# Deformable preact block on one Trainium2 core: the deform stage on four bands of whole rows

## The chip, the cores and the metric

The kernel runs on one core of a Trainium2 chip. The metric is the device time of one execution in microseconds (us). The core has TensorE (PE: matmuls, with its weight loads shown as PEld), VectorE (DVE), ScalarE (ACT), GpSimd (POOL), and SyncE (SP), which here only issues DMAs; ScalarE issues a few as well. A "q" behind an engine's name in a row (SPq, ACTq) is that engine's sequencer, busy with issuing a DMA.

## The reference, cut to what matters

The input is 8 images of 32 channels, 128 x 128, fp32. Two residual layers follow each other:

```
x = x + pointwise/attention mixes of depthwise3x3(gn(x))      # one 3x3 convolution once the weights are folded
x = x + conv3x3(deform(gn(x)), w_conv) + b_conv

deform(x): off = conv3x3(x, w_off)           # 64 channels: (row, column) offsets
           rows, cols = clip(grid + off)     # own pixel plus an offset
           bilinear mix of the pixels (floor, ceil) of rows and cols
```

`gn` is a normalization with as many groups as channels: one mean and one variance for each channel of each image. The kernel folds it into the weights and a bias, so that every padding pixel must hold the channel's mean. As long as every offset is below 1 in size, the bilinear mix needs only the own pixel, its neighbour above or below and its neighbour at the left or right; a general path, which these inputs don't take, stands behind the fast one.

## The kernel before

Each image is stored as `[128 partitions, 32 or 33 blocks, 130 columns]`: partition 32*q + c holds channel c of the image rows 4*b + q, b being the block. Three such tiles (`x1a`, used in turn) hold the result of the first convolution, `x1b` the same shifted by two rows (one convolution needs both, each matmul contracts four rows of 32 channels), `xa` and `xb` the input of the first convolution, `mapa` and `mapb` the deformed image, input of the second. A convolution of an image is 8 groups of 4 blocks. [...]

The program goes over images i = 0 to 7, and in each over 8 chunks k. In chunk k TensorE computes the offsets of one eighth of image i (`offsets`, L715, 24 records), and behind them the jobs that `jobs_behind` lists: groups of the first convolution of image i+1 (`conv1_groups`, at chunks 0 to 3), and the eight groups m = 0 to 7 of the second convolution of image i-1 (`LAST_CONV2`: one behind chunk 3, one behind chunk 4, two behind each later chunk). `CONV2_GROUPS` says which group of blocks the m-th is. All these jobs share three PSUM banks in turn, so a job waits for the bank to be emptied three jobs earlier. The jobs before the last image keep this order; the last image has its own (`END_CONV2`, `END_GROUPS`).

The deform stage of chunk k runs through three engines. Its input is `x1_quads`: the image cut in four quarters (left or right half, upper or lower half), one for each 32 partitions, with one row of neighbours around. ScalarE copies row differences and column neighbours into place (`offset_parts`, L909 and L911), waits for the offsets, and writes their positive parts and absolute values (L920 to L924); VectorE selects and multiplies (`deform`, L1317 to L1329); GpSimd adds up (L1115 to L1127) and writes `mapped`, then computes the row differences for the chunk after next (`row_steps`, L1101). So chunk k needs, on ScalarE, what GpSimd did behind chunk k-2. TensorE may start the offsets of chunk k when VectorE is done with chunk k-2 (`off_used`).

SyncE moves the data between these layouts, in one queue and in the order of the code:

- `copy_x1b` (L402): `x1a` into `x1b`, shifted, 520 KB each, two for each half of the image
- `move_quads` (L336): `x1a` into `x1_quads`, 16 DMAs for each half, rows of 65 or 64 elements
- `move_mapa` (L407): `mapped` into `mapa`, 16 DMAs for each half, rows of 64 elements
- `copy_mapb` (L417): `mapa` into `mapb`, two for each half, once `move_mapa` of that half has landed
- `load_xb` (L392), the input of image i+2, 8 DMAs; `store` (L364), 5 and 4 DMAs

Within image i the order is: `copy_x1b` half 1, `copy_mapb` half 0, `store` part 1, `move_quads` half 1, `move_mapa` half 1, `copy_mapb` half 1, `load_xb`, then for the next image `copy_x1b` half 0 and `move_quads` half 0, then `move_mapa` half 0 and `store` part 0. The conv2 jobs wait at m = 0 for half 0 of `mapb` and at m = 2 (chunk 5, block group 0) for half 1 (L675).

The padding columns are written by ScalarE: in `x1a` and `x1b` (`pad_x1`, L811) and in `mapa` (`pad_map`, L828). The mean comes from `x1_norm` on VectorE, which stands ahead of the chunk that follows the last first-convolution group. `clamp` (L935) repeats the edge rows and columns in `x1_quads`. For the last image the lower quarter rows don't go by DMA: `end_row` copies (L298) on VectorE, ScalarE and GpSimd write `xa` and `xb` in two parts.

## Time and profile before

| | us |
|---|---|
| median of 3 runs | 739.05 (738.85 to 739.9) |
| the profiled execution, its own time | 740.63 |
| its span, first to last instruction | 738.8 |
| TensorE busy | 690.1 (93%) |
| VectorE, ScalarE, GpSimd busy | 519.5, 475.7, 491.6 |
| mean granted TensorE clock | 0.981 |
| DMA packets | 240878, of which 140880 under 512 B |

The page is one profiled execution. Busy times are unions of an engine's instructions. A row of a timeline begins with its start and its length in us; "[4.13 <-DMA ...]" is idle time of the engine just before, and what ended it. A row of windows gives busy time and, in brackets, instructions for each engine, then the granted clock as a share of 2.4 GHz.

### The profile page before, as it was taken

Reading aid. Unit: us, or ns where it says so; the run is one execution under the profiler, and the core shown is the slowest. Engines: PE = TensorE matmul, PEld = TensorE weight load, DVE = VectorE, ACT = ScalarE, POOL = GpSimd, SP = SyncE. Lnnn points to the kernel's source line nnn. Section 1 sums busy time; section 2 is a strip of 40 time slices with the busy share of each in tenths; the row PEclk is TensorE's granted clock in tenths of the full one; section 3 lists DMA queues with packets and bytes.
Section 4 is the critical chain, followed back from the end, with each engine's and each line's share of the span. In section 5 each row is a group of like instructions: output and inputs, shape, how many; then the busy total and the mean of one; then the engine's idle time right before and its main releaser. Section 6 shows DMA issues by size and latency. Waiting matters only on the chain. (4 is left out here: it accounts for less than half of the span.)

```text
span 738.8 us, 10814 instructions
## 1 busy us (share of the span) xinstructions
PE 690.1 (93%) x3500; PEld 247.4 (33%) x3500; DVE 519.5 (70%) x1031; ACT 475.7 (64%) x841; POOL 491.6 (67%) x434
## 2 busy tenths in 40 slices
PE   4799989999999889998999979999899999997966
PEld 4333333333333233333333333333333333332322
DVE  3687996598954886749955698566985595657592
ACT  7487867785675836676467654667576674876560
POOL 4004968879687486766686575857766849699650
PEclk9999989999999989999999999999999999999998
DMA  8969904999789894989959799696968563657554
GB/s 141 186 102 148 177 10 104 205 145 197 136 195 180 148 200 104 232 146 170 184 133 238 133 166 166 155 220 122 204 127 190 140 148 66 160 109 166 133 123 112
DMA packets 240878, 113.08 MB, mean 153 GB/s; under 512 B 140880, under 2 KB 235184, under 8 KB 239024
## 3 DMA queue, kind: packets, MB, share of 16 engines
q1 hardware_dynamic: 216784, 100.55, 71.0%
q10 hardware_dynamic: 24032, 11.78, 8.4%
q8 instruction: 29, 0.48, 0.3%
q14 instruction: 33, 0.27, 0.1%
HBM read 31.59 MB, written 16.78 MB: 65 GB/s over the span
## 5 line engine op out<-in xcount | busy, mean ns | idle before, releaser
L1317 DVE COPY_PREDICATED other_row<-down_ps,row_diff 128x768 f32<-128x768 int32 x128 | 124.4, 1024 | 139.4 <-ACT down_ps L920 139.1
L715 PE MATMUL off_ps<-x1a,wo 128*64 128x512 f32 x768 | 178.9, 601 | 2.1 <-DVE other_row L1329 2.1
L1115 POOL TENSOR_TENSOR other_row<-other_row,x_quads 128x512 f32<-128x512 f32 x64 | 76.3, 1193 | 154.2 <-DVE other_row L1329 154.2
L715 PE MATMUL off_ps<-x1b,wo 128*64 128x512 f32 x768 | 175.9, 593 | 0.0
L606 PE MATMUL c_ps<-xb,w 128*64 128x512 f32 x336 | 150.8, 598 | 5.6 <-DVE x1a L1301 5.5
L606 PE MATMUL c_ps<-mapb,w 128*64 128x512 f32 x336 | 151.7, 595 | 0.0
L608 PE MATMUL c_ps<-xa,w 128*64 128x512 f32 x336 | 150.8, 598 | 0.0
L909 ACT ACTIVATE other_row<-row_diff 128x768 f32<-128x768 f32 x128 | 101.7, 843 | 68.2 <-POOL row_diff L1101 63.0
L608 PE MATMUL c_ps<-mapa,w 128*64 128x512 f32 x294 | 132.7, 595 | 0.0
L1101 POOL TENSOR_TENSOR row_diff<-x_quads 128x594 f32<-128x594 f32 x64 | 79.5, 1243 | 43.7 <-ACT x_quads L945 43.7
L920 ACT ACTIVATE down_ps<-off_ps,bias_o 128x512 f32<-128x512 f32 x64 | 41.7, 652 | 84.1 <-PE off_ps L715 75.6
L715 PEld LDWEIGHTS off_ps<-x1b,wo 128*64 128x64 f32 x768 | 55.5, 136 | 110.2 <-issue 110.2
L715 PEld LDWEIGHTS off_ps<-x1a,wo 128*64 128x64 f32 x768 | 54.4, 138 | 103.7 <-issue 100.7
L1121 POOL TENSOR_TENSOR other_col<-other_col,off_abs 128x512 f32<-128x512 f32 x64 | 83.0, 1297 | 5.0
L1118 POOL TENSOR_TENSOR other_col<-other_col,other_row 128x512 f32<-128x512 f32 x64 | 81.8, 1279 | 5.0
L1127 POOL TENSOR_TENSOR mapped<-other_col,other_row 128x512 f32<-128x512 f32 x64 | 81.8, 1278 | 5.0
L1116 POOL TENSOR_TENSOR other_col<-other_col,other_row 128x512 f32<-128x512 f32 x64 | 81.9, 1280 | 0.0
L606 PEld LDWEIGHTS c_ps<-xb,w 128*64 128x64 f32 x336 | 45.3, 137 | 100.7 <-issue 94.3
L606 PEld LDWEIGHTS c_ps<-mapb,w 128*64 128x64 f32 x336 | 44.7, 136 | 90.5 <-issue 89.9
L932 ACT ACTIVATE beyond<-off_abs,minus_one 128x1024 bf16<-128x1024 f32 x64 | 73.0, 1140 | 0.1
L922 ACT ACTIVATE off_abs<-off_ps,bias_o 128x1024 f32<-128x1024 f32 x64 | 70.7, 1105 | 0.0
L1274 DVE BATCH_NORM_STATS2 stats<-x1a 128x6 f32<-128x512 f32 x64 | 42.1, 683 | 24.3 <-ACT x1a L868 24.3
(134 smaller groups left out, 970.4 us busy)
## 6 DMA issues: line engine op xcount, KB each, us to landing
x1b<-x1a SPq DMA_DIRECT2D x28, 520.0 KB, 7.6
mapb<-mapa SPq DMA_DIRECT2D x28, 520.0 KB, 6.9
mapa<-mapped SPq DMA_DIRECT2D x224, 64.0 KB, 2.1
out_dram<-x1a SPq DMA_DIRECT2D x49, 256.0 KB, 4.7
x_quads<-x1a SPq DMA_DIRECT2D x192, 65.0 KB, 3.1
xb<-in_x_dram SPq DMA_DIRECT2D x48, 256.0 KB, 8.1
xa<-in_x_dram ACTq DMA_DIRECT2D x40, 256.0 KB, 6.8
xa<-in_x_dram SPq DMA_DIRECT2D x16, 256.0 KB, 6.9
```

The source lines that it names most:

```text
L606: nc.tensor.matmul(bank[0:64, :], weights[:, kx, :], rows_b[:, 4 * g:4 * g + 4, kx:kx + W], start=(kx == 0), stop=(kx == 2))
L608: last = nc.tensor.matmul(bank[64:128, :], weights[:, kx, :], rows_a[:, 4 * g:4 * g + 4, kx:kx + W], start=(kx == 0), stop=(kx == 2))
L715: last = nc.tensor.matmul(off_ps[k % 2][64 * t:64 * t + 64, CH * n:CH * n + CH], wo[wpar][:, kx, 64 * t:64 * t + 64], rows[:, 4 * k:4 * k ...
L909: act.activation(other_row[n][:, :, KR // 2 * odd:KR // 2 * odd + KR // 2, :], every_other_3(row_diff[n], odd), ACT.Copy)
L932: act.activation(beyond[:, :], off_abs[k % 2][:, :], ACT.Relu, bias=minus_one[:, :], accum_out=far[i % 2][:, k:k + 1]).then_inc(beyond_rea ...
L1101: pool.tensor_tensor(row_diff[n][:, :, :], x1_quads[:, KR * k + 1:KR * k + KR + 2, :], x1_quads[:, KR * k:KR * k + KR + 1, :], ALU.subtrac ...
L1115: step(pool.tensor_tensor(split(column), split(column), own, ALU.add))
L1116: step(pool.tensor_tensor(side, side, other_row[n][:, 0, :, :], ALU.add))
L1118: step(pool.tensor_tensor(side, side, column, ALU.subtract))
L1121: step(pool.tensor_tensor(side, side, off_abs[n][:, 1:2 * CH:2].rearrange("p (h w) -> p h w", h=KR), ALU.mult))
L1127: pool.tensor_tensor(by_pairs(mapped, KR * k, 0), split(side), split(column), ALU.add).then_inc(mapped_ready, 1)
L1317: last = dve.copy_predicated(other_row[n][:, :, KR // 2 * odd:KR // 2 * odd + KR // 2, :], bass.AP(tensor=rows.tensor, offset=rows.offset ...
```

## The change

- `x1_quads` becomes `x1_strips`: four bands of 32 whole rows, one for each 32 partitions, half 0 (rows 0 to 15 of each band) in one buffer and half 1 in two that take turns. Rows are stored by remainder modulo 4, so that each of the 16 DMAs of a half moves one contiguous run of 4 or 5 whole rows with their pads (520 B each) for each partition. The rows' pads must be written before: `copy_x1b` and the strips of image i+1 now wait for `x1_pads` of that image, and `pad_x1` moves to the chunk behind the first convolution's last group.
- A chunk is now 8 rows by one half of the width: chunks 0 to 3 are rows 0 to 15 of all bands, 4 to 7 the others. Both halves' strips of image i+1 are issued in one go of 32 DMAs during image i, ahead of `move_mapa` half 0; none is left between the last chunk and `move_mapa` half 1.
- `mapped` has the layout `[4 rows, 8 blocks, 130]` and carries the pad columns (`pad_mapped`), so `move_mapa` moves 2080 B runs. Its halves are now blocks 0 to 3 and 4 to 7 of each band.
- For images 0 to 5, conv2's m = 0 waits for both halves of `mapb`, and the order is block groups 0, 2, 4, 6, 1, 3, 5, 7. For images 6 and 7 a group is 4 blocks 8 apart; m = 0 needs half 0 and m = 3 half 1.
- `row_steps` computes the differences of two chunks in two instructions (128x792 and 128x330), behind each even chunk; ScalarE waits for both.
- `SECOND_CONV1` puts the last two conv1 groups behind chunks 2 and 3 in place of both behind chunk 2.
- At the end, five conv2 groups of image 6 stand in the chunks (seven before), three behind them (one before). For image 7, three groups need half 0; the other five need the left columns by DMA and one part of `end_row` copies (12 ScalarE, 10 GpSimd, 10 VectorE).
- Biases use 64-column sums, and some small tiles lie in spare room of the strips. The scratch for GpSimd's own DMAs is cut; this kernel issues none there.

```diff
-    SECOND_CONV1 = [[3], [4, 5], [6, 7], [], [], [], [], []]
+    SECOND_CONV1 = [[3], [4, 5], [6], [7], [], [], [], []]
-    END_CONV2 = [[], [], [0], [1], [], [2, 3], [4, 5], [6]]
-    CONV2_GROUPS = [1, 5, 0, 4, 2, 6, 3, 7]
-    STORE_AFTER = [7, 8]
-    END_GROUPS = [1, 5, 2, 6, 3, 0, 4, 7]
-    END_PARTS = [0, 0, 1, 1, 2, 2, 2, 2]
+    END_CONV2 = [[], [], [0], [1], [2], [3], [4], []]
+    CONV2_GROUPS = [0, 2, 4, 6, 1, 3, 5, 7]
+    STORE_AFTER = [6, 8]
+    BEFORE_END_GROUPS = [1, 2, 3, 0, 4, 5, 6, 7]
+    END_GROUPS = [1, 2, 3, 4, 5, 6, 7, 0]
+    END_PARTS = [0, 0, 0, 1, 1, 1, 1, 1]
@@ SyncE
                 if prev:
                     sp.wait_ge(mapped_ready, NK * i)
-                    move_quads(sp, i % 3, 1)
                     if i >= 2:
                         sp.wait_ge(conv2_done, 8 * (i - 1))
+                    sp.wait_ge(mapped_pads, 2 * i)
                     move_mapa(1)
                     sp.wait_ge(mapa_moved[1], A_MOVES * DMA * i)
                     copy_mapb(1)
...
-                    sp.wait_ge(x1_ready, 8 * (i + 1) + 5)
+                    sp.wait_ge(x1_pads, i + 2)
                     sp.wait_ge(off_done, NK * i + 4)
                     copy_x1b((i + 1) % 3, 0)
-                    sp.wait_ge(x1_ready, 8 * (i + 1) + 8)
-                    sp.wait_ge(mapped_ready, NK * i + 5)
-                    move_quads(sp, (i + 1) % 3, 0)
+                    sp.wait_ge(mapped_ready, NK * i + 4)
+                    for half in range(2):
+                        move_strips(sp, i + 1, half)
...
+                    move_rows(xa, 0, 4, end_moved[0])
+                    sp.wait_ge(end_moved[0], A_MOVES * DMA)
+                    copy_rows(xb, xa, 0, 4, end_copied[0])
+                    sp.wait_ge(mapped_pads, 2 * i + 2)
+                    sp.wait_ge(mapped_ready, NK * i + 6)
+                    move_left_columns(end_moved[1])
+                    sp.wait_ge(end_moved[1], A_MOVES * DMA)
+                    copy_rows(xb, xa, 4, 4, end_copied[1])
@@ TensorE
-                if m in (0, 2):
+                halves = [m // 3] if spread(i) and m in (0, 3) else range(2) if not spread(i) and m == 0 else []
+                for half in halves:
@@ ScalarE
-                act.wait_ge(diff_ready, g + 1)
+                act.wait_ge(diff_ready, 2 * (g // 2 + 1))
...
+                    if nxt and k and 7 in conv1_groups(i, k - 1):
+                        pad_x1(i + 1, (i + 1) % 3)
@@ GpSimd
+                pool.tensor_tensor(diff[:, 0:12 * WQP].rearrange("p (q j w) -> p q j w", q=3, j=4),
+                                   rows(PLANE, inner), rows(0, inner), ALU.subtract).then_inc(diff_ready, 1)
+                pool.tensor_tensor(diff[:, 12 * WQP:17 * WQP].rearrange("p (j w) -> p j w", j=5),
+                                   rows(0, [[WP, 5]]), rows(strip_row(-1), [[WP, 5]]),
+                                   ALU.subtract).then_inc(diff_ready, 1)
...
-                    if k + 2 < NK:
-                        row_steps(i, k + 2)
-                    elif i + 1 < NB:
-                        row_steps(i + 1, k + 2 - NK)
+                    if k % 2 == 0 and k < NK - 2:
+                        row_steps(i, k // 2 + 1)
+                    elif k == NK - 2 and i + 1 < NB:
+                        row_steps(i + 1, 0)
@@ VectorE
+            def copy_end_rows():
+                dve.wait_ge(end_copied[1], B_MOVES * DMA)
+                dve.wait_ge(mapped_ready, NK * NB)
...
             for m in range(8):
-                if m == 2:
-                    copy_end_rows(1)
+                if m == COPY_END_BEFORE:
+                    copy_end_rows()
```

`COPY_END_BEFORE` is 3. The strips of one band:

```python
STRIP_PLANES = ((0, 0, 5), (1, 0, 4), (2, 0, 4), (3, -1, 5))
def move_strip(queue, i, half, strip):
    par, to = i % 3, strips_of(i, half)
    p_to = Q * (2 * (strip % 2) + strip // 2)
    for q, first, n in STRIP_PLANES:
        p, b = (Q * (q + 1), NJ * strip + 4 * half + first) if q < 3 else (0, NJ * strip + 4 * half + first + 1)
        at = PLANE * q + WP * first
        if i > 0:
            queue.dma_start(to[p_to:p_to + Q, at:at + n * WP],
                            x1a[par][p:p + Q, b:b + n, :].rearrange("p b w -> p (b w)")).then_inc(strips_loaded[half], DMA)
```

## Rows read from the trace of the kernel before

**Rows 1.** The page's part 1, busy time of each engine

```profile
PE 690.1 (93%) x3500; PEld 247.4 (33%) x3500; DVE 519.5 (70%) x1031; ACT 475.7 (64%) x841; POOL 491.6 (67%) x434
```

**Rows 2.** TensorE's waits: who waited for whom, total us, times, longest

```profile
PE c_ps L616 <- DMA mapb<-mapa: 15.5, 6, 4.1
PE c_ps L633 <- DVE w L1270: 8.2, 2, 5.1
PE c_ps L606 <- DVE x1a L1301: 5.5, 1, 5.5
```

**Rows 3.** Windows: busy PE, PEld, DVE, ACT, POOL (instructions), granted clock, DMA, GB/s

```profile
261.00:271.00 10.00, 10.00 (x54) 4.10 (x48) 7.98 (x14) 2.12 (x3) 9.61 (x9) 0.72 1.26 198
...
437.00:442.00 5.00, 5.00 (x32) 2.45 (x26) 4.89 (x8) 0.00 (x0) 4.84 (x5) 0.66 1.25 191
```

**Rows 4.** TensorE's timeline around the second convolution's groups, images 1, 4, 5 and 6

```profile
157.08 0.59 PE L606 MATMUL c_ps<-mapb,w 128*64 128x512 f32 x1
...
416.61 0.59 PE L606 MATMUL c_ps<-mapb,w 128*64 128x512 f32 x1
...
436.36 0.48 PE L616 MATMUL c_ps<-mapb,w 128*32 128x384 f32 x1 [4.13 <-DMA mapb<-mapa]
...
505.83 0.59 PE L606 MATMUL c_ps<-mapb,w 128*64 128x512 f32 x1
...
591.33 0.59 PE L606 MATMUL c_ps<-mapb,w 128*64 128x512 f32 x1
```

**Rows 5.** SyncE's timeline from 440 to 530 us, one period of its queue

```profile
442.66 14.53 SPq L349 DMA_DIRECT2D x_quads<-x1a  x16
457.28 11.64 SPq L414 DMA_DIRECT2D mapa<-mapped  x16
...
485.64 13.24 SPq L349 DMA_DIRECT2D x_quads<-x1a  x16
...
516.72 0.62 SPq L425 DMA_DIRECT2D mapb<-mapa  x1
```

**Rows 6.** By line: L414's issue times (min/median/max ns), L414's and L425's landing times

```profile
L414 SPq DMA_DIRECT2D mapa<-mapped x224: 585/611/1875, 118.6 to 665.8; - x112
...
DMA to landing us min/median/max: 2.1/2.1/7.3
...
DMA to landing us min/median/max: 6.5/7.6/11.4
```

**Rows 7.** Timelines of VectorE and ScalarE around chunk 3 to 4 of image 4

```profile
422.78 0.73 DVE L1301 SCALAR_TENSOR_TENSOR x1a<-c_ps,bias,x1a 128x512 f32<-128x512 f32 x1
...
426.86 1.14 ACT L932 ACTIVATE beyond<-off_abs,minus_one 128x1024 bf16<-128x1024 f32 x1
```

**Rows 8.** Timelines of GpSimd, ScalarE and VectorE in image 0

```profile
72.33 1.23 POOL L1101 TENSOR_TENSOR row_diff<-x_quads 128x594 f32<-128x594 f32 x1
...
76.50 1.94 DVE L1317 COPY_PREDICATED other_row<-down_ps,row_diff 128x768 f32<-128x768 int32 x2
...
86.50 1.28 POOL L1127 TENSOR_TENSOR mapped<-other_col,other_row 128x512 f32<-128x512 f32 x1
...
105.27 0.66 ACT L920 ACTIVATE down_ps<-off_ps,bias_o 128x512 f32<-128x512 f32 x1 [5.76 <-PE off_ps L715]
```

**Rows 9.** Timelines of TensorE, GpSimd and VectorE in the last image

```profile
632.93 2.75 PE L715 MATMUL off_ps<-x1a,wo 128*64 128x512 f32 x12
635.51 2.75 PE L715 MATMUL off_ps<-x1b,wo 128*64 128x512 f32 x12
...
649.05 1.27 POOL L1127 TENSOR_TENSOR mapped<-other_col,other_row 128x512 f32<-128x512 f32 x1
...
710.52 0.40 POOL L1138 COPY xb<-mapped 32x256 f32<-32x256 f32 x1
...
711.52 0.43 DVE L1385 TENSOR_SCALAR xa<-mapped,ones 32x256 f32<-32x256 f32 x1
...
732.43 0.20 PE L738 MATMUL c_ps<-far_image,ones 128*1 128x8 f32 x2 [0.92 <-DVE far_image L1398]
```

455 lines of the change are left out of this document (233 added, 222 removed).

## The prediction, on record before the changed kernel was run

> **What bounds the kernel now.** I read the page's busy times first: TensorE works 690.1 of 738.8 us [rows 1], so a change gains only where TensorE waits. Its waits by releaser come next [rows 2]: six waits, 15.5 us in all, for `mapb`, always at L616, block group 0, which is m = 2 behind chunk 5; two, 8.2 us, for the scaled weights of the first convolution at the start; one of 5.5 us near the end. Then the clock, window by window: after the 4.1 us wait of image 2 the granted clock is 0.72 of 2.4 GHz for 10 us, after that of image 4 it is 0.66 for 5 us [rows 3]. TensorE was fully busy there, so these cost 10 x 0.28 = 2.8 us and 5 x 0.34 = 1.7 us more. Last the timeline [rows 4]: m = 0 of the second convolution starts at 416.61 in image 4 and at 505.83 in image 5, 89.2 us apart; less the wait of 4.13 and 1.7 of slow clock a period of TensorE's own work is 83.4 us. From 157.08 (image 1) to 591.33 (image 6) are 434.2 us, five periods are 417.0, so 17.2 us are lost in images 1 to 5. That is what the change can reach in the middle of the kernel.
>
> Why `mapb` is late is in SyncE's queue [rows 5]. From `move_quads` half 0 at 442.66, which the strips replace, to `copy_mapb` half 1 (second issue at 516.72, landed some 6.7 us later, 523.4) are 80.8 us with scarcely a pause: 16 moves in 14.5, 16 in 11.6, then stores and copies until 485.64, then 16 and 16 more. An issue takes 0.61 us whatever the size [rows 6], 0.65 with the gap. The chain then starts anew only after the 8 loads of x and `copy_x1b`. So SyncE's queue is as long as TensorE's period, and the wait is its excess.
>
> **The steady images.** *Removed:* the 16 moves between chunk 7 and `move_mapa` half 1, 13.2 us [rows 5]. *Moved:* they now stand ahead of `move_mapa` half 0, so the queue holds the same 64 moves and they come only from one place to another. Each is still an issue of 0.65 us. What is saved is the queueing: 14.5 and 11.6 us for 16 where 10.4 is the bare price. I take 32 strips at 20.9 us. *Moved earlier:* both halves of `mapb` are needed at m = 0, behind chunk 3, instead of the second at m = 2, behind chunk 5. That is two groups and two chunks of offsets sooner: a group is 12 records and starts 2.57 us before what follows it (the two halves of a chunk's offsets start 2.58 apart [rows 9]), so 2 x 2.57 + 2 x 5.15 = 15.4 us.
>
> *Added:* SyncE waits for `x1_pads` before `copy_x1b`, with the strips, `move_mapa`, stores and all the rest queued behind it. The pads stand on ScalarE behind chunk 4's parts, and the mean they use comes from `x1_norm`, which on VectorE stands behind the addition of m = 0 (that order can be seen at 422.78, where L1301 is followed by the norm [rows 7]). So a loop closes: m = 0, its addition and the norm, pads, SyncE's queue, `mapb`, the next m = 0. Its length decides. Let S be the start of m = 0:
> - group 0 takes 2.7, chunk 4's offsets 5.2, ScalarE's parts 2.5, `sum_far` 1.3 (from 424.5, the end of those offsets, `sum_far` starts at 426.86 [rows 7]), three pads 0.9: S + 12.7. VectorE's mean is ready before (0.7 addition, 2.7 norm).
> - two issues of `copy_x1b` 1.3, strips 20.9, `move_mapa` half 0 10.4: S + 45.3.
> - stores, `copy_x1b` half 1, `copy_mapb` half 0, as now from 468.9 to 485.64: 16.7 [rows 5]: S + 62.0.
> - `move_mapa` half 1 10.5, last landing 2.1 after its issue at best, 7.3 at worst [rows 6]; loads of x by ScalarE fall here, I take 3.6: S + 75.5.
> - `copy_mapb`: second issue 0.7 later, landing 6.5 at best, 7.6 the median [rows 6], I take 6.8 as before a load of x: S + 83.0.
> TensorE comes back to m = 0 at S + 83.4. The loop fits by 0.4 us. With landings at their worst it is 3 to 4 us too long, with issues slightly cheaper it is 2 short. I take 0.4 us of waiting for each of images 2 to 6, 2 us in all, bounds 0 and 15. Waits this short leave the clock alone: of the 17.2 us now lost, waits are 12.7 (15.5 less the last image's 2.8 [rows 2]) and the two slow stretches 4.5, so the short waits of images 1, 3 and 5 cost no clock.
>
> **Image 1.** Here the queue starts late. Before, `copy_x1b` for image 1 went out at chunk 4 of image 0; now it waits for pads behind chunk 5. ScalarE's parts of chunk 5 start at 105.27 [rows 8]; I add 1.2 (below), 2.5 parts, 0.3 for the new `pad_mapped`, 1.3 `sum_far`, 0.9 pads: 111.4. Then 1.3, strips 20.9, `move_mapa` half 0 10.4: 144.0; `copy_x1b` 1.3, landing, `copy_mapb` half 0 1.5: 146.8; no stores yet; `move_mapa` half 1 10.5 and landing 1.5: 158.8; `copy_mapb` 0.7 + 6.5: 166.0. TensorE wants m = 0 at 157.08 [rows 4] + 1.2 = 158.3 (the new `SECOND_CONV1` leaves that place where it is). So a wait of 7.7 us that was 0.5, and a slow clock behind it: 2.8 by [rows 3] (1.7 the other bound). Image 1 costs 10.5 us.
>
> **Image 0 and the pairs.** ScalarE's copies for an even chunk wait for two differences instead of one. A difference of 594 elements takes 1.23 [rows 8]; 792 and 330 elements in proportion 1.65 and 0.7, so the pair is ready 1.1 us later than the one is now. Where the deform stage runs without slack the way from `mapped` of chunk k-2 to that of chunk k is 72.33 to 87.78, 15.4 us [rows 8]; it becomes 16.6 for two chunks. Chunk 2 of image 0 has it once before `x_norm` of image 2, so the first wait for weights (3.1 of the 8.2 [rows 2]) grows by 1.2 us. GpSimd's work doesn't grow (2.35 for two chunks against 2.46), and in images 1 to 6 a chunk of TensorE is 10.3 us or more, which hides it; if that cover is gone it is 0.6 us a chunk. *Edits with one answer, no cost:* strips in other layouts (same elements), 64-column bias sums, pads in `mapped` (2 x 0.3 on ScalarE, which has slack), `clamp` of half 1 no longer waiting for its DMA.
>
> **The last image**, T being its first offsets, 632.93, and TensorE's end about 731.5, T + 98.6 [rows 9]. `mapped` of chunk 0 ends at T + 17.4 [rows 9]. With 16.6 a pair chunk 5 is ready at T + 17.4 + 33.2 + 8.8 = T + 59.4. Then 16 left columns 10.4, landing 1.5, `copy_rows` 0.7 + 6.4 at the low end of the landings: T + 78.5. Now the end copies: ScalarE's 12 at 0.43 are 5.1; GpSimd's 10 at 0.40 and VectorE's 10 at 0.43 beside each other [rows 9] are 4.4. Group 4 of 8 starts at T + 83.8. Before it TensorE has been idle some 10 us, where it waited 5.5 [rows 2]. Five groups, 4 x 2.57 + 2.7 = 13.0, and 2.8 of slow clock: T + 99.6. That is 1.0 later than now; between 97 and 103, as landings go. What I count here replaces the waits that the last image has now (2.8 for `mapb`, 2.1 for VectorE, and the 5.5).
>
> One rule speaks against the shared end copies: the Trainium skill, SBUF — State Buffer, "SBUF: two separate sides", says that VectorE in a two-port mode and GpSimd hold one port pair by an exclusive lock for a whole instruction. By that the two shares of ten would add up to 8.3 us, 3.2 over the 5.1 of ScalarE. In this trace a GpSimd copy (0.40) and a VectorE copy (0.43) ran side by side in the same stretch, so the trace doesn't bear it out for these copies.
>
> **The sum**, against the span of 738.8: -17.2 (images 1 to 5), +10.5 (image 1), +2.0 (images 2 to 6), +1.2 (image 0), +1.0 (last image) = -2.5, a span of 736.3. The profiled execution took 740.63 by its own time, 1.8 above its span, and the runs' median is 739.05; 739.05 - 2.5 gives 736.5 us.
>
> **The rivals.**
> - *The loop is longer than TensorE's period.* The mechanism is the one above: `copy_x1b` waits for pads that wait for m = 0. It decides from a loop of 83.4 us. For it: landings of `move_mapa` reach 7.3 and of `copy_mapb` 11.4 [rows 6], and ScalarE's loads fall right there. Against it: the strips are short runs no more, and the queue gets 5 us of rest before. With 86 us in each of five images, 2.6 us each, 13 for 2, it is 747.5; 750 if one wait drags the clock down. Chance 0.28. This one is slower than before.
> - *The queue gets shorter than counted.* Moves of one run for each partition could issue below 0.61, say at 0.55; 64 of them and 48 in image 1's way save 3.5 us in each loop: images 2 to 6 wait nothing (-2), image 1 3 less, the tail 1 less: 730.5. For it: only that quads with many rows took up to 14.5 for 16. Against: `mapa` moves take 0.61 in all their 224. Chance 0.14.
> - *The wait moves and nothing else.* The 17.2 us come back as image 1's and small waits in full: 739. Chance 0.10.
> - *The lock of the shared port pair holds* in the end copies: the 3.2 us above lengthen the idle stretch before the last five groups, 739.7. Chance 0.02.
>
> **How the numbers follow.** Forecast 736.5 with chance 0.46, its own range 732.5 to 741. A measurement tells about 0.2% from no change, so 737.6 to 740.5 counts as the same. Faster: 0.14, and two thirds of 0.46, 0.31: 0.45. Same: the third left of it less what passes 740.5, 0.12, and 0.10 and 0.02: 0.24. Slower: 0.28 and 0.03: 0.31. The range 729 to 749 leaves out the far ends of the two outer cases, 0.2 together.
>
> **What would show it.** Right: no wait at L616 for images 2 to 6, or below 1 us; one wait of 6 to 9 us at the first group of image 1's m = 0, with a lower clock behind it; 32 strips in a row in about 21 us; an idle TensorE of about 10 us in the last image; m = 0 to m = 0 in 83.4 to 84 us. Wrong: periods above 85 us with `mapb` as releaser each time (the loop), waits of TensorE for VectorE's L1329 in images 0 or 7 (the pairs), or issues of strips far from 0.61 us.

## The result and the profile after

The changed kernel takes 779.23 us (median of 5 runs, 775.46 to 779.66), the kernel before 739.36 beside it (5 runs, 738.85 to 740.16): a ratio of 1.0528, 95% interval 1.0502 to 1.0553. The forecast was 736.5 with a range of 729 to 749; it was wrong in sign and in size. The execution that was profiled took 775.46 us, the lowest of the five (that of the kernel before 740.63), so the trace shows 34 to 35 us of the loss and not the whole 40.

The page's busy times and the waits of the kernel after (waiting engine and line, releaser, total us, times, longest) answer to [rows 1] and [rows 2]. L662 is the first group of m = 0, L651 any other group, L448 is `copy_x1b`, L842 a pad, L1364 the addition of m = 0, L1065 an end copy:

```profile
PE 697.6 (90%) x3500; PEld 249.3 (32%) x3500; DVE 507.7 (66%) x1017; ACT 458.5 (59%) x792; POOL 491.0 (63%) x434
...
DVE x1a L1364 <- PE c_ps L670: 54.1, 7, 16.5
...
PE c_ps L662 <- DMA mapb<-mapa: 34.9, 6, 15.0
...
PE c_ps L651 <- ACT xb L1065: 8.3, 1, 8.3
...
SPq L448 <- ACT x1a L842: 78.6, 7, 26.0
```

TensorE waits for `mapb` at each of the six m = 0, 34.9 us in all, and 2.6 us once more in the last image; before it was six waits with 15.5 us in all, at m = 2. New is the last line: ahead of `copy_x1b` SyncE stands still for the pads, 78.6 us in all. Of this 26.0 are in image 0 (where before it stood still for 23.2 us too, for `mapped`), and 5.3 to 10.8 in each of images 1 to 5. In these its queue isn't full, it is held up.

TensorE's timeline at the first group of m = 0, images 1 to 6, against [rows 4]:

```profile
176.77 0.82 PE L662 MATMUL c_ps<-mapb,w 128*32 128x384 f32 x1 [15.04 <-DMA mapb<-mapa]
...
267.81 0.82 PE L662 MATMUL c_ps<-mapb,w 128*32 128x384 f32 x1 [5.65 <-DMA mapb<-mapa]
...
357.15 0.48 PE L662 MATMUL c_ps<-mapb,w 128*32 128x384 f32 x1 [3.39 <-DMA mapb<-mapa]
...
445.81 0.48 PE L662 MATMUL c_ps<-mapb,w 128*32 128x384 f32 x1 [3.46 <-DMA mapb<-mapa]
...
536.56 0.82 PE L662 MATMUL c_ps<-mapb,w 128*32 128x384 f32 x1 [5.58 <-DMA mapb<-mapa]
...
624.66 0.48 PE L662 MATMUL c_ps<-mapb,w 128*32 128x384 f32 x1 [1.75 <-DMA mapb<-mapa]
```

The six starts split the loss into three parts (TensorE's last matmul ends at 732.63 before and 766.91 after):

| | before | after | measured | forecast |
|---|---|---|---|---|
| start to m = 0 of image 1 | 157.1 | 176.8 | +19.7 | +8.9 |
| from there to m = 0 of image 6 | 434.2 | 447.9 | +13.7 | -12.4 |
| from there to TensorE's end | 141.3 | 142.2 | +0.9 | +1.0 |
| sum | | | +34.3 | -2.5 |

(Forecast of the second line: -17.2, + 2.8 for the clock behind image 1's wait, + 2.0.) The last image came out as forecast, the other two did not. A period is 88.1 to 91.0 us where TensorE's own work is 83.4.

Windows behind the waits, as in [rows 3] (busy time of PE, PEld, DVE, ACT, POOL, granted clock, DMA, GB/s):

```profile
176.00:181.00 5.00, 4.23 (x28) 2.14 (x29) 0.00 (x0) 0.00 (x0) 0.00 (x0) 0.54 1.24 197
...
267.00:277.00 10.00, 9.19 (x50) 4.06 (x52) 3.05 (x16) 1.50 (x3) 1.91 (x2) 0.71 1.26 185
...
445.00:451.00 6.00, 5.18 (x34) 2.63 (x36) 0.63 (x2) 2.10 (x3) 5.04 (x4) 0.72 1.26 195
```

In the 5 us with the end of the 15.0 us wait TensorE was granted 0.54 of 2.4 GHz (most of that time the level of 1.2), in the 6 us with the end of the 3.5 us wait 0.72. In the first two stretches VectorE, ScalarE and GpSimd have little or nothing to do: the whole chain of engines has run dry behind m = 0.

One round of SyncE's queue, from image 3's m = 0 at 357.15 to image 4's at 445.81, against [rows 5]:

```profile
371.39 0.61 SPq L448 DMA_DIRECT2D x1b<-x1a  x1
...
372.69 23.89 SPq L375 DMA_DIRECT2D x_strips<-x1a  x32
396.69 10.18 SPq L456 DMA_DIRECT2D mapa<-mapped  x16
406.91 2.27 SPq L407 DMA_DIRECT2D out_dram<-x1a  x3
...
411.94 0.90 SPq L448 DMA_DIRECT2D x1b<-x1a  x1
...
413.76 1.72 SPq L469 DMA_DIRECT2D mapb<-mapa  x1
...
417.82 5.67 SPq L407 DMA_DIRECT2D out_dram<-x1a  x3
...
424.17 12.11 SPq L456 DMA_DIRECT2D mapa<-mapped  x16
437.69 0.65 SPq L469 DMA_DIRECT2D mapb<-mapa  x1
...
439.06 15.66 SPq L438 DMA_DIRECT2D xb<-in_x_dram  x8
460.01 0.60 SPq L448 DMA_DIRECT2D x1b<-x1a  x1
```

The round can be read off leg by leg, with the forecast's terms beside it:

| leg | measured | forecast |
|---|---|---|
| m = 0 to `copy_x1b` (357.15 to 371.39) | 14.2 | 12.7 |
| its two issues, to 372.69 | 1.3 | 1.3 |
| 32 strips, to 396.69 | 24.0 | 20.9 |
| `move_mapa` half 0, to 406.91 | 10.2 | 10.4 |
| stores, `copy_x1b` half 1, `copy_mapb` half 0, to 424.17 | 17.3 | 16.7 |
| `move_mapa` half 1 and its landing, to 437.69 | 13.5 | 13.5 |
| `copy_mapb` half 1, to m = 0 of the next image at 445.81 | 8.1 | 7.5 |
| round | 88.7 | 83.0 |

The first leg on ScalarE in the round that starts at 445.81: parts of chunk 4, `sum_far`, pads, and SyncE's 460.01 above follows at once:

```profile
455.61 0.66 ACT L966 ACTIVATE down_ps<-off_ps,bias_o 128x512 f32<-128x512 f32 x1 [8.42 <-PE off_ps L762]
...
457.92 1.14 ACT L978 ACTIVATE beyond<-off_abs,minus_one 128x1024 bf16<-128x1024 f32 x1
...
459.06 0.92 ACT L842 ACTIVATE x1a<-dve_columns 128x66 f32<-128x66 f32 x3
```

Chunk 4's offsets are there 9.8 us behind m = 0; 7.9 were counted. The low clock behind the wait makes them late, so the wait lengthens the loop that causes it. The other images show by how much. Behind image 6's m = 0, which waited only 1.75 us, the granted clock is 1.00 and `copy_x1b` follows after 12.5 us (624.66 to 637.20), as forecast; at a clock of 0.72 (images 3 and 4) it follows after 14.2, at 0.51 (image 5) after 15.4.

### The profile page after: what moved, and what is told of

It reads as the page before. It is cut to its first block, busy times and chain, and to the rows that moved or that the text cites. A ratio compares the mean times of both kernels' runs of the same rounds, so it can differ in the third digit from the quotient of the medians.

```text
span 773.5 us, 10713 instructions
## 1 busy us (share of the span) xinstructions
PE 697.6 (90%) x3500; PEld 249.3 (32%) x3500; DVE 507.7 (66%) x1017; ACT 458.5 (59%) x792; POOL 491.0 (63%) x434
## 4 chain that ended last, share of the span: by engine, by line
SPq 45%; PE 14%; DMA 9%; POOL 6%; issue 4%; ACT 4%; DVE 3%; ACTq 0%; POOLq 0%; DVEq 0%
SPq L456 16%; SPq L375 15%; PE off_ps L762 7%; DMA mapb<-mapa 5%; SPq L407 5%; PE c_ps L651 4%; DMA mapa<-mapped 2%; SPq L469 2%; SPq L470 2%; PE c_ps L662 2%; PE c_ps L666 2%; SPq L410 1%; SPq L479 1%; SPq L448 1%; POOL other_col L1182 1%
## 5 line engine op out<-in xcount | busy, mean ns | idle before, releaser
L1176 POOL TENSOR_TENSOR other_row<-other_row,x_strips 128x512 f32<-128x512 f32 x64 | 76.1, 1190 | 185.3 <-DVE other_row L1392 185.3
L651 PE MATMUL c_ps<-xb,w 128*64 128x512 f32 x336 | 151.1, 599 | 8.3 <-ACT xb L1065 8.3
L651 PE MATMUL c_ps<-mapb,w 128*64 128x512 f32 x336 | 151.9, 598 | 2.6 <-DMA mapb<-mapa 2.6
L651 PEld LDWEIGHTS c_ps<-xb,w 128*64 128x64 f32 x336 | 45.5, 137 | 103.8 <-issue 103.5
L651 PEld LDWEIGHTS c_ps<-mapb,w 128*64 128x64 f32 x336 | 45.3, 137 | 95.0 <-issue 95.0
L1160 POOL TENSOR_TENSOR row_diff<-x_strips 128x792 f32<-128x792 f32 x32 | 51.1, 1597 | 38.3 <-ACT x_strips L997 38.3
```

The costliest lines, as they stand in the source:

```text
L651: nc.tensor.matmul(bank[0:64, :], weights[:, kx, :], rows_b[:, of, kx:kx + W], start=(kx == 0), stop=(kx == 2))
L1176: step(pool.tensor_tensor(split(column), split(column), own, ALU.add))
```

## The experiments

**Theory 1**, the loop: m = 0 waits for both halves of `mapb`; pads (and on VectorE the norm) wait for m = 0; SyncE waits for the pads; and `mapb` waits for SyncE. **Theory 2**, the rival: SyncE's queue is too long by itself, and the wait for the pads only fills what is left. Kernels are named by their labels. "Period" is m = 0 to m = 0.

### The loop cut at the pads, and cut at the demand

`e1_norm_first`:

```diff
@@ VectorE, behind the statistics of a chunk's conv1 groups
-                    if nxt and k and 7 in conv1_groups(i, k - 1):
-                        x1_norm(i + 1, (i + 1) % 2, (i + 1) % 3)
...
                             x1_stats(i + 1, (i + 1) % 3, m)
+                        if 7 in conv1_groups(i, k):
+                            x1_norm(i + 1, (i + 1) % 2, (i + 1) % 3)
...
@@ ScalarE
-                    if nxt and k and 7 in conv1_groups(i, k - 1):
+                    if nxt and 7 in conv1_groups(i, k):
                         pad_x1(i + 1, (i + 1) % 3)
```

> The changed kernel, with x1_norm placed on VectorE behind the statistics of group 7 and ahead of the addition of m = 0, and pad_x1 on ScalarE at the end of the same chunk (chunk 3 in the middle images, chunk 4 in image 0) in place of the next one. Nothing else moves. The pads then no longer depend on m = 0. Theory 1 (the loop: m = 0, its addition, the norm, pads, copy_x1b, strips, mapb, next m = 0): the start of m = 0 no longer drives SyncE. In the changed kernel SyncE was free at 454.73 and sent copy_x1b only at 460.01, so the loop falls from 88 to 91 us to what SyncE's own queue takes, 83 to 84, which is also TensorE's own period: m = 0 of image 1 to m = 0 of image 6 takes 417 to 425 us, was 447.9, and image 1's m = 0 comes some 8 to 11 us earlier than 176.8, since the pads of image 1 come a chunk earlier. Time about 740, range 735 to 750. Rival (SyncE's queue is too long by itself, its issues and landings being slower than counted, and the wait for pads only fills the rest): periods stay at 88 us or more, the SyncE wait for the pads goes and the wait shows up elsewhere; time 768 or more in the middle images' part, with image 1's gain at the most 765.

Measured: 745.19 us (ratio 1.0075, 1.0054 to 1.0097), 34 us below the changed kernel. Image 1's m = 0 starts at 173.2, the periods are 85.2 and then four times 83.4. Of this kernel, a window over the middle images and then SyncE's timeline:

```profile
240.00:580.00 340.00, 340.00 (x1760) 118.24 (x1758) 251.00 (x494) 220.54 (x380) 243.22 (x196) 1.00 0.88 179
```

```profile
416.60 10.74 SPq L438 DMA_DIRECT2D xb<-in_x_dram  x8
430.82 0.60 SPq L448 DMA_DIRECT2D x1b<-x1a  x1
...
432.27 20.81 SPq L375 DMA_DIRECT2D x_strips<-x1a  x32
```

TensorE is busy 340.00 of 340 us at full clock: where nothing waits for m = 0, the middle images have no loss at all. Theory 1 holds there. Image 1's part was missed: 3.6 us gained where 8 to 11 were expected, since in image 0 VectorE is late with the norm (ScalarE stands still for it until 105.3) and the pads come only 3 us sooner (`copy_x1b` at 106.3 for 109.3).

`e2_spread_all`:

```diff
-        return isinstance(i, int) and NB - 2 <= i < NB
+        return isinstance(i, int) and i < NB
-    STORE_AFTER = [6, 8]
+    STORE_AFTER = [8, 8]
```

> The changed kernel, with the second convolution's groups of images 0 to 5 formed as for images 6 and 7 (4 blocks 8 apart, order 1, 2, 3, 0, 4 to 7): m = 0 needs half 0 of mapb alone and m = 3 half 1, and the first part of an image's store waits for all 8 groups. The pads still stand behind m = 0. Theory 1 (the loop, and within it the demand for half 1 of mapb at m = 0): half 0 of mapb has landed at 417.8 or so and m = 0 never waits; m = 3 comes 18 us behind m = 0, when half 1 has landed (some 87 us behind the m = 0 before, against 83.4 + 18). Image 1 starts m = 0 at 161 to 163 (was 176.8), the five periods fall from 88 to 91 to 83.4 to 84 us (m = 0 of image 1 to 6: 417 to 421, was 447.9), the clock stays up. Time 779 - 15 - 29 = 735, range 729 to 740, which is below the kernel before. Rival (the queue is too long by itself, however the demand is placed): the wait goes from m = 0 to m = 3 and the periods stay at 86 us or more; 750 to 770.

Measured: 748.97 us (1.0136, 1.0098 to 1.0175), above the 729 to 740 named. Image 1's m = 0 starts at 162.9, and no m = 0 waits for `mapb`, with the pads still behind m = 0. So the loop is also cut at the demand. But the periods are 88.7, 84.5, 88.6, 84.6, 85.9, not 83.4 to 84, and this kernel's waits name a new cause:

```profile
ACT x1a L911 <- DMA out_dram<-x1a: 58.0, 5, 12.9
PE c_ps L651 <- ACT x1a L914: 10.4, 5, 3.5
```

ScalarE may not write `x1a` anew before the store has landed, and a spread group touches every part of the image, so nothing can be stored before the eighth. The time is 14 us above the 735 expected; the periods together are 15 above 417, so that is the likely place of it.

### Six issues more, inside the loop and outside

`e3_in_loop` and `e4_off_loop` add the same six small DMAs at two places:

```diff
+                    for e in range(6):
+                        sp.dma_start(extra[:, 6 * i + e:6 * i + e + 1], conv_b.rearrange("(c o) -> c o", o=1)).then_inc(extra_in, DMA)
                     copy_x1b((i + 1) % 3, 0)          # e3: between the wait for the pads and copy_x1b
...
                     copy_mapb(1)                      # e4: behind this, ahead of the loads of x
```

> The changed kernel, with 6 small DMAs (32 numbers each, into an unused corner) issued by SyncE in each of images 0 to 6 right behind the wait for the pads and ahead of copy_x1b half 0. 6 issues of 0.6 us are 3.7 us. Theory 1 (the loop through the pads): they lie in the loop, so image 1's m = 0 is 3.7 us later and each of the five periods 3.7 us longer (91 to 94.5), m = 0 of image 1 to 6 takes 466 us, was 447.9; time 779 + 22 = 801, or up to 805 with the last image. Rival (queue too long by itself): the same here, 801; it differs in the next run. If SyncE isn't what sets the end: no change, 779.

> The changed kernel, with the same 6 small DMAs in each of images 0 to 6, now issued right behind copy_mapb half 1 and ahead of the loads of x, before SyncE comes to the wait for the pads (where it idles 5.3 us in image 4 and 18 in image 6). Theory 1 (the loop through the pads): they fill the idle time, and copy_x1b goes out when the pads come, as without them: no change, 779, at most 784 where some image has less than 3.7 us of idle time there. Rival (the queue is too long by itself): 6 issues more are 3.7 us in every period, wherever they stand: 801 as in the run before.

Measured: 809.78 us inside (ratio 1.0949; 801 to 805 were expected), 776.46 outside (1.0499), the changed kernel being 1.0528. Each of the two ran twice. In the loop the periods are 98.5, 94.8, 91.9, 96.1, 91.5; outside 91.3, 89.0, 88.0, 90.4, 88.4, as without them.

The six issues in SyncE's timeline, first inside the loop, then outside it:

```profile
479.16 2.64 SPq L542 DMA_DIRECT2D x1a<-in_L_conv_b_conv_dram  x6
```

```profile
438.76 5.95 SPq L534 DMA_DIRECT2D x1a<-in_L_conv_b_conv_dram  x6
```

Off the loop the six issues took 5.95 us and cost nothing; in it they took 2.64 and cost 5.0 a period. That speaks against theory 2 for the changed kernel: its queue has room. The test is less clean than it looks, though. Off the loop the 8 loads of x behind the six issues took 10.72 us, where they take 15.66 in the changed kernel, so, counted from image 4's m = 0, SyncE came to its wait for the pads only 1.4 us later, and it still stood still there for 3.5. What bears the argument is that SyncE waits for the pads in every image in both runs, together with the cuts of the loop above and at the end. Nor does the loop through the clock explain why the price inside is 5.0 and not 2.64: the way from m = 0 to the pads is 13.9 to 15.4 us there and 14.2 to 15.4 in the changed kernel. In the period of 96.1 `copy_mapb` half 1 landed 11.1 us behind its first issue, where it takes 8.0 in the changed kernel, and three other legs are 0.5 to 0.7 us longer; why wasn't settled.

### The demand alone, in the kernel before

`f4_before_need`:

```diff
                 if m in (0, 2):
                     images = i + 1 if isinstance(i, int) else i
-                    for half in [m // 2] if isinstance(i, int) else range(2):
+                    for half in range(2):
```

> The kernel before, with one edit: m = 0 of the second convolution waits for both halves of mapb (before: m = 0 for half 0, m = 2 for half 1). In the kernel before half 1 lands 19.6 us behind the start of m = 0 (436.2 against 416.6 in image 4's timeline). Theory 1 (the place of the demand is paid in full and a loop closes behind it): SyncE's move_quads half 0 waits for chunk 4 of the deform stage, which stands behind m = 0 on TensorE, some 20 us behind its start; from there 80.8 us to half 1's landing, so the period is about 101 us where it was 87, and image 1's m = 0 is some 15 us later: 740 + 15 + 5 x 14 = 825, range 790 to 840. Rival (the queue catches up: the later demand costs its 15 to 20 us once, and the periods stay at 84 to 90 us): 755 to 765.

Measured: 827.32 us (1.1191, 1.1141 to 1.124), periods 97.3, 98.8, 98.7, 98.5, 92.4. SyncE's timeline shows the second issue of `copy_x1b` at 375.14 and then a standstill until chunk 4 is mapped:

```profile
375.14 0.60 SPq L405 DMA_DIRECT2D x1b<-x1a  x1
392.71 7.25 SPq L349 DMA_DIRECT2D x_quads<-x1a  x11
```

So the later demand isn't paid once, as a shift. It closes a loop in the old kernel too, through another wait. That 825 was forecast and 827 measured is luck in part: image 1's m = 0 is 16.6 us later (15 forecast), the five periods are together 51.5 longer (70 forecast), and 20.5 come in the last image, where m = 0 waits 22.8 us, which the forecast left out. The changed kernel has no such demand in its last image. At the other two places the demand costs 68 us here, and the changed kernel loses 33: the rest of the change gives back about half.

### What else holds when the demand is split

All three stand on `e2_spread_all` with the store's second part directly behind its first:

```diff
-                if nxt and i >= 2:
-                    sp.wait_ge(out_ready, 8 * (i - 1))
-                    store(sp, i - 2, (i - 2) % 3, 1)
...
                     store(sp, i - 1, (i - 1) % 3, 0)
+                    store(sp, i - 1, (i - 1) % 3, 1)
```

`f5_spread_stores` is that, `f6_spread_norm` adds the edit of `e1_norm_first`, `f7_spread_groups` adds `SECOND_CONV1 = [[3], [4, 5], [6, 7], ...]`.

> The changed kernel with the second convolution's groups spread for all images (as in the run with m = 0 needing half 0 of mapb and m = 3 half 1), and the second part of an image's store issued right behind the first in place of behind copy_mapb half 0 of the next image. In the run with spread groups alone m = 0 never waited for mapb, but ScalarE waited 58 us in five places for the store's landing ahead of writing x1a anew, and TensorE 10.4 us for ScalarE, so the periods were 88.7, 84.5, 88.6, 84.6, 85.9. Theory 1 (with the demand split, nothing of the deform side sets the period; what was left is the late store): the second part lands 10 us sooner (231 where it was 241), ScalarE's write of group 4 in chunk 2 doesn't wait, periods 83.4 to 84.5, m = 0 of image 1 at 163; TensorE's end about 725 (was 737.6), time 733, range 729 to 738, below the kernel before. Rival (the first part, for group 0 in chunk 0, is what is late, since it now waits for all 8 groups): periods stay at 88 and 84.5, time 746 to 750.

> As the run before (spread groups for all images, stores together), and besides x1_norm and pad_x1 at the end of the chunk with the last group of the first convolution, as in the first run. Theory 1: moving the pads helped by 30 us in the first run only because m = 0 waited for half 1 of mapb and so held the pads; where m = 0 doesn't wait, the same move changes nothing: within 2 us of the run before. Rival (early pads are worth something by themselves, as SyncE starts 12 us sooner): 3 to 6 us faster than the run before. Against both: ScalarE stands still for the mean ahead of the next chunk's copies, which may cost 1 us a period where ScalarE is late.

> As the run with spread groups and stores together, with SECOND_CONV1 as in the kernel before (groups 6 and 7 behind chunk 2 of image 1). Theory (the 2.8 us wait for the second convolution's weights at the bias job of image 1, and the offsets at half clock behind it, come from group 7 having been moved from ahead of that job to behind chunk 3): the wait vanishes or is below 0.5 us, the offsets behind it take 5.3 in place of 7.1 us, image 1's m = 0 starts at 158 to 159 in place of 162.9, time 4 us less than that run. Rival (VectorE is late there by the pairs of differences, whatever TensorE's order): a wait of 2 to 3 us stays in image 1.

Measured: 752.40 us (1.0168, 1.0135 to 1.0202), 745.72 (1.0083, 1.0052 to 1.0115) and 747.71 (1.0136, 1.009 to 1.0182). `f5` fell (733 expected, 746 to 750 by its rival): TensorE's waits for ScalarE are 5.6, 4.8 and 2.7 us in images 2, 4 and 6. It is the first part that is late, as its rival had it; that the store behind it delays the rest of the queue would explain the time above the rival's, but its interval overlaps that of `e2_spread_all`. `f6` is 6.7 us faster than `f5` where theory 1 said nothing would change: early pads give something of their own even where no m = 0 waits for `mapb`, so the rival (3 to 6) was right there. `f7` did what was expected at its place: the wait of 2.4 us for the scaled weights before chunk 3 is gone and image 1's m = 0 starts at 158.2 (161.8 in `f5`); the median is 4.7 lower, with four runs each and intervals that overlap. But a wait of 2.6 for VectorE ahead of the offsets behind m = 0 came up in its place, so of the 3.6 us part went again.

### Towards a version faster than before

`h1_norm_narrow` is `e1_norm_first` with another end:

```diff
-                    copy_rows(xb, xa, 4, 4, end_copied[1])
+                    copy_left_columns(sp, False)       # 4 DMAs of 65 columns; act issues the other 4
...
-                    pe.wait_ge(end_copied[1], B_MOVES * DMA)
+                    pe.wait_ge(end_copied[1], 8 * DMA)
...
-            act.wait_ge(end_copied[1], B_MOVES * DMA)
+            act.wait_ge(end_moved[1], A_MOVES * DMA)
+            copy_left_columns(act, True)
...
-            pool.wait_ge(end_copied[1], B_MOVES * DMA)
...
-                dve.wait_ge(end_copied[1], B_MOVES * DMA)
...
-    COPY_END_BEFORE = 3
+    COPY_END_BEFORE = 2
```

`h2_two_spread` adds spread groups for images 0 and 1 and the old `SECOND_CONV1`, `h3_one_spread` the same for image 0 alone.

> The changed kernel with the first run's edit (x1_norm ahead of the addition of m = 0, pad_x1 in the same chunk), and at the end the copy from xa to xb behind the left columns moves those 65 columns alone, in 8 DMAs (4 issued by SyncE, 4 by ScalarE) in place of 2 of whole rows. So the end_row copies no longer wait for that DMA: in the first run the last mapped was there at 707.0 and the copies ran from 713.0 to 718.5, with TensorE waiting 9.5 us until 718.57. Theory: GpSimd and VectorE copy from 707 to 712, ScalarE from 708.4 (behind its 4 issues) to 713.6, the 8 DMAs land by 711 to 712, and TensorE resumes at 713.6 in place of 718.6: 5 us, time 745.2 - 5 = 740, range 738 to 742. Rival (8 small DMAs with 260 byte runs land later than 2 large ones, 6 us or more behind the last issue): TensorE resumes at 716 or later, 743 or more.

> As the run before, with spread groups for images 0 and 1 too (as for 6 and 7; their first store part waits for all 8 groups) and SECOND_CONV1 as in the kernel before. In the first run only image 1's m = 0 still waited, 14.2 us; the middle images ran at 83.4 us a period. Theory: image 1's m = 0 starts at 158 in place of 173.2 (as in the runs with all images spread), image 2's at 247 to 250 (ScalarE's wait for the late store costs 3 to 4 us, as there), image 3's at 332 to 336, limited by SyncE's 83 us a round, where it was 341.9; then 83.4 each. 6 to 9 us less than the run before: time 733, range 730 to 737, below the kernel before. Rival (SyncE's queue, once behind, sets image 2's and 3's mapb whatever TensorE does before): m = 0 of image 3 stays at 341 to 342 and the time within 2 us of the run before.

> As the run before, but with spread groups for image 0 alone. Image 1's m = 0 starts at 158, but image 2's needs both halves of mapb, which landed at 255.4 in the first run: it starts at 253 to 256 in place of 258.4 after a wait of 8 us or more, so of the 15 us gained in image 1 only 3 to 5 are kept: 740 - 4 = 736, range 734 to 739. Rival (the 15 us are kept): 727.

Measured: 741.06 us (1.002, 1.0 to 1.0039), 742.55 (1.0036, 1.0016 to 1.0057), 740.16 (1.002, 1.0 to 1.0041). `h1` came as expected: TensorE resumes at 714.27 in place of 718.57, 4.3 of the 5 us. The other two missed (733 and 736 expected). Image 1's m = 0 starts at 158 in both, and the 15 us are gone two images later: m = 0 of image 3 stands at 343.6 and 342.6 (`e1`: 341.9). SyncE's timeline of `h3_one_spread` at image 2, with theory 2 in plain sight:

```profile
249.70 16.18 SPq L448 DMA_DIRECT2D xb<-in_x_dram  x8
...
267.90 24.15 SPq L375 DMA_DIRECT2D x_strips<-x1a  x32
```

With no idle time left, SyncE needs 86 to 87 us a round: more than 83.4. So behind the loop there is a second limit some 2 us lower, and theory 2 is true of a kernel in which the loop is cut and SyncE is behind. In `e1` the same instructions took 10.74 (with a pause of 3.3 in it) and 20.81 us.

### Is an issue dear because of what is in flight?

`k1_after_rest` (on the changed kernel), `k2_one_spread_rest` (on `h3`) and `k3_two_spread_rest` (on `h2`) add one wait:

```diff
                 if after and prev:
+                    sp.wait_ge(mapb_copied[1], B_MOVES * DMA * i)
                     for half in range(2):
                         sp.wait_ge(conv1_done, 8 * (i + 1) + (5 if half == 0 else 8))
                         load_xb(i + 2, half, xb_loaded)
```

> The changed kernel with one added wait on SyncE: ahead of the loads of x (load_xb) it waits until copy_mapb half 1 has landed, some 7 us. The loads now take 14.7 to 15.9 us for 8 issues right behind it. Theory (issues are stretched while large transfers of the same queue are in flight; the loop through the pads sets the period): the 8 issues take 4 to 8 us after the rest, SyncE comes to the wait for the pads at about the same time as now and the period stays at 88 to 91 us: 777 to 781. Rival (an issue of a load has a fixed price near 1.9 us): SyncE comes 2 to 3 us too late in every image, 779 + 13 = 792.

> As the run with spread groups for image 0 (pads early, 65 column copies at the end, SECOND_CONV1 as before), with the added wait ahead of the loads of x. There SyncE took 86.2 to 86.8 us a round with no idle time, mapb half 1 landed at 256.3 and 342.5, and TensorE waited 6.1 and some 3 us for it. Theory (stretched issues): resting 6.6 us and then issuing 8 loads in 4 to 7 us ends 3 to 5 us sooner than 16.2 us without rest, and the strips behind fall from 24 to 21: half 1 lands at 253 to 255 in image 2 and at 334 to 337 in image 3, m = 0 of image 6 at 587 in place of 593: time 740 - 5 = 735, range 732 to 738, below the kernel before. Rival (the rest is idle time and nothing else): SyncE's round grows by up to 6.6 us in images 1 and 2, time 744 or more.

> As the run with spread groups for images 0 and 1, with the added wait. There image 3's m = 0 waited 11.4 us for half 1 of mapb, landed at 343.5. Theory: half 1 lands at 334 to 336 and m = 0 of image 3 starts then, where it was 343.6; m = 0 of image 6 at 588 where it was 596.7; time 742.5 - 8 = 734.5, range 731 to 738. Rival (idle time and nothing else): 746 or more.

Measured: 782.63 us (1.0598, 1.0561 to 1.0635; two runs), 749.82 (1.0136, 1.0092 to 1.0181), 748.39 (1.0141, 1.0111 to 1.0172). The same place in SyncE's timeline of `k2_one_spread_rest`:

```profile
257.15 9.16 SPq L448 DMA_DIRECT2D xb<-in_x_dram  x8
...
268.28 24.18 SPq L375 DMA_DIRECT2D x_strips<-x1a  x32
```

The first half of the theory holds: after the rest the 8 issues take 9.16 where they took 16.18. The second doesn't: they end at 266.31 where they ended at 265.88, and the strips behind are as slow as before. The rest bought in issue time what it cost in idle time. In the later images, where the loads weren't stretched, it made SyncE late again: the last three periods, 83.4 each in `h3_one_spread`, are 86.8, 86.3 and 85.4, which is 8 of the 10 us that `k2` loses. `k3` missed too (734.5 expected): in its profiled execution, the fastest of six with 743.43 us, m = 0 of image 3 starts at 343.3, as in `h2_two_spread`, and where the 6 us of its median went doesn't show there. In `k1_after_rest` the 8 loads take 9.2 to 11.0 us in images 2 to 5, where they took 14.7 to 15.9 (4 to 8 were expected), the periods are those of the changed kernel (91.2, 89.2, 89.1, 91.2, 88.8) and the time is 1.6 us above the range named; the rival's 792 is ruled out. So about a third of that issue time was waiting time, not work.

### The loop cut at SyncE's wait

`l2_bare_strips` is the changed kernel, `l1_first_strips` is `h1_norm_narrow`, with the strips of all images or of image 1 alone moved without their pad columns (runs of 512 B), ahead of the wait and of `copy_x1b`:

```diff
-                if i > 0:
+                if i > 7:                              # l1: i > 1
                     queue.dma_start(to[p_to:p_to + Q, at:at + n * WP],
...
+                    if i + 1 <= 7:                     # l1: i + 1 <= 1
+                        sp.wait_ge(x1_ready, 8 * (i + 1) + 8)
+                        sp.wait_ge(mapped_ready, NK * i + 4)
+                        for half in range(2):
+                            move_strips(sp, i + 1, half)
                     sp.wait_ge(x1_pads, i + 2)
                     sp.wait_ge(off_done, NK * i + 4)
                     copy_x1b((i + 1) % 3, 0)
...
+                    if not i + 1 <= 7:                 # around the old place of the strips
```

> The kernel with early pads and the 65 column copies (741.06 us), and image 1's strips moved without their pad columns (runs of 512 B, as image 0's already are), issued when the first convolution of image 1 is done and chunk 3 mapped, ahead of the wait for the pads and of copy_x1b half 0. Theory: mapped of chunk 3 ends at 97.3, so the strips go out at 97.4 where they went at 107.8 to 108.6; the whole of SyncE's way to mapb half 1 is 10 to 11 us earlier, image 1's m = 0 starts at 162 to 164 after a wait of 3 to 5 us (was 173.4 after 14.2), the stretch of low clock behind it shortens, the later periods stay at 83.4: time 741 - 10 = 731, range 728 to 735, below the kernel before. Rival (shorter runs cost it: 32 strips of 512 B runs take 30 us or more, or move_mapa half 0 waits for mapped chunks anyway): m = 0 at 168 or later, 737 or more.

> The changed kernel (norm and pads where it has them, no other edit), with the strips of all images moved without their pad columns, ahead of SyncE's wait for the pads; copy_x1b half 0 behind them. Theory (the loop through the pads): SyncE goes on at once, in image 4 at 454.7 where it waited until 460.0, so the period falls to what the queue takes without idle time, 84 to 87 us, and image 1's m = 0 starts 10 us sooner, at 165 to 167: m = 0 of image 1 to 6 in 420 to 433 where it was 447.9; time 779 - 10 - 15 to 28 = 741 to 754. Rival (the period is set by something else that moved with the norm in the first run, VectorE's or ScalarE's order): periods stay at 88 to 91, time 768 or more.

Measured: `l2_bare_strips` 741.36 us (1.0046, 1.0027 to 1.0066), image 1's m = 0 at 166.4, periods 87.6, 84.1, 83.9, 84.2, 83.4. The norm and the pads stand where the changed kernel has them; only SyncE's wait no longer holds the strips, and 38 us are gone. Three cuts at three places of the loop give 30 to 38 us, and issues added in it cost time while outside they don't: the loop is shown. The shorter runs and the place ahead of `copy_x1b` came with this cut; the strips of images 1 to 7 together took 8.6 us less than in the changed kernel, far from 38.

`l1_first_strips` takes 734.17 us against 738.37, a ratio of 0.9931 (0.9908 to 0.9954): 0.7% faster than the kernel before, beside which it ran. Its SyncE timeline in image 0 and TensorE's at its first two m = 0:

```profile
97.80 21.27 SPq L381 DMA_DIRECT2D x_strips<-x1a  x32
119.17 0.68 SPq L458 DMA_DIRECT2D x1b<-x1a  x1
```

```profile
165.35 0.82 PE L678 MATMUL c_ps<-mapb,w 128*32 128x384 f32 x1 [3.29 <-DMA mapb<-mapa]
...
252.71 0.48 PE L678 MATMUL c_ps<-mapb,w 128*32 128x384 f32 x1 [1.03 <-DMA mapb<-mapa]
```

The strips start at 97.80 for 109.92 in `h1_norm_narrow`, and image 1 waits 3.3 us for 14.2. The gain is 7 us of the 10 expected: m = 0 came at 165.35, just behind the 162 to 164 named.

## Why the prediction was wrong, step by step

- **What bounds the kernel before.** Right: TensorE's own period is 83.4 us. `e1_norm_first` runs four periods of it with no loss.
- **"The loop fits by 0.4 us."** This is the step that failed. The loop was named, with all its legs, and its sum was 83.0; it is 88.7. Of the 5.7 us missing, 3.1 are the strips, 1.5 the way to the pads, 0.6 the stretch of stores and copies and 0.6 the last landing (`move_mapa` half 0 was 0.2 cheaper). Behind the strips' term stands a choice: 0.65 us for an issue, the bare price, though the same section said that 16 quads took 14.5 us and 16 `mapa` moves 11.6. The quads of [rows 5] took 4.1 and 2.8 us more than the bare 10.4. The excess of the strips sits in their first two issues (below), so it comes once for a group and not once for an issue: 20.9 and 2.8 to 4.1 are 23.7 to 25.0 us, 24.0 measured, and the loop is then 86 to 87, which is too long already. The rows that were to give the bound had the answer, and I reasoned them away. (In the sum the 10.5 and 3.6 us of `move_mapa` half 1 are 13.5 together, since a landing counts from the start of its issue.)
- **The shape of the cost.** I charged the excess over 83.4 once per image. But the excess is a wait, the waits of 3.4 to 5.7 us were followed by a clock of 0.51 to 0.72, and the way to the pads took 14.2 to 15.4 us in place of 12.5, so a loop that is too long by some 3.6 us becomes one too long by 5.3. "Waits this short leave the clock alone" held for 0.4 us, and for the 1.75 us of image 6, but the loop didn't stay at them.
- **The demand at m = 0.** I costed it as 15.4 us earlier, on a queue that had to meet it, and never added it up alone. `f4_before_need` did: image 1's m = 0 came 16.6 us later, as such a shift would, but the mean period went from 86.8 to 97.2 us. The change does that with one hand and has to give more than that back with the other.
- **Image 1.** `mapb` was forecast at 166.0 and landed at 176.6, though `copy_x1b` went out at 109.3, 2.1 sooner than counted. The queue took 67.3 us where I had 54.6: strips 24.5 for 20.9, `copy_mapb` half 0 and what is with it 5.7 for 2.8, `move_mapa` half 1 with its landing (behind ScalarE's loads of x) 18.2 for 12.0. The first two are the same error as above; of the third, 2.4 us are dearer issues and the rest is the landing. The slow clock behind it, forecast at 2.8 us, cost some 2 (the period of 91.0 less the next wait of 5.65 and 83.4).
- **"The new `SECOND_CONV1` leaves that place where it is."** Wrong. The bias job before chunk 3 waits 2.94 us for the second convolution's weights, since group 7 no longer stands ahead of it, and chunk 3's offsets then run at a low clock. `f7_spread_groups` takes it away: 3.6 us of image 1's 19.7.
- **Image 0 and the pairs.** Right: the wait for weights before chunk 5 grew from 3.12 to 4.00 us, by 0.9; 1.2 were forecast.
- **The last image.** Right: TensorE's last group ends 99.3 us behind its first offsets (forecast 99.6), the idle stretch is 8.3 (forecast about 10). In part two errors cancel: 2.6 us of waiting for `mapb` stayed in this image, which the sum had at nothing.
- **The rivals.** The first one, at 0.28, is what happened, mechanism and place, but its price was 2.6 us an image and 747.5 to 750. It measured 5.3 in the round shown and 6.2 on average, and image 1's 19.7 were in no case at all. The range ended at 749 because each case took one error at a time; the strips' price is in image 1's way and in every period together. The queue shorter than counted: no, the median issue of a strip is 0.59 us, but they reach 2.3. The lock of the port pair: its price of 3.2 us didn't come. The end copies of the kernel after, VectorE's and then GpSimd's timeline:

```profile
745.63 0.43 DVE L1449 TENSOR_SCALAR xa<-mapped,ones 32x260 f32<-32x260 f32 x1
```

```profile
745.50 0.40 POOL L1200 COPY xb<-mapped 32x260 f32<-32x260 f32 x1
```

Both engines copy every 0.44 us beside each other and are done with their shares after 4.3 and 4.4 us, where the prediction's sum by the lock was 8.3. But the prediction concluded too much from [rows 9], that the trace doesn't bear out the rule. These are the same VectorE copies in the kernel before, with the GpSimd instruction beside the first of them:

```profile
707.40 1.29 POOL L1121 TENSOR_TENSOR other_col<-other_col,off_abs 128x512 f32<-128x512 f32 x1
...
707.48 1.35 DVE L1385 TENSOR_SCALAR xb<-mapped,ones 32x256 f32<-32x256 f32 x1
...
716.34 0.34 DVE L1385 TENSOR_SCALAR xb<-mapped,ones 32x256 f32<-32x256 f32 x1
```

A copy takes VectorE 0.34 us while GpSimd does nothing, 0.42 to 0.44 beside GpSimd's copies of 0.40, and 1.33 to 1.35 beside GpSimd instructions of 1.26 to 1.29. So VectorE does wait for the GpSimd instruction beside it, and the rule of the Trainium skill that was weighed (SBUF — State Buffer, "SBUF: two separate sides") agrees with this trace. What was wrong is adding up whole recorded durations: beside copies as short as these the price is 0.1 us a copy.

## What to carry to other kernels

Where a change makes a queue wait for something that stands behind the consumer of what the queue delivers, write the loop down and sum it at the prices that the rows show for such a stretch, not at the price of one issue with nothing around it. A loop that fits by less than the spread of its own terms can't be counted as fitting: here it paid its excess in every round and lowered the clock besides. To tell a loop from a full queue, put the same few issues once inside it and once outside, and see in the trace whether the idle time or the neighbours' issues made room for them; and look for the cheapest cut, which here was not to shorten the queue but to let 32 moves go without waiting for two columns.
